# A state-space layer and a linear attention on one core: one ring for states and products, carries by four, steps re-placed, the chunk loop written out

## The chip, the cores and the metric

The kernel runs on one core of one Trainium2 chip. The metric is the device time of one execution in microseconds (us), median of the runs shown. The core has TensorE (PE, with its weight loads as PEld), VectorE (DVE), ScalarE (ACT), GpSimd (POOL) and SyncE (SP), which here only issues DMAs. Each engine works through its own list of instructions in order and waits on semaphores.

## The reference

Input x is 2 images of 512 channels by 4096 tokens, float32. Two layers follow each other, each added to its input:

```
x = x + mamba(group_norm(x))
x = x + linear_attention(group_norm(x))
```

The first layer, per token t, with 1024 inner channels d and 16 states n:

```
xn = layer_norm(x);  xin, z = split(xn @ in_proj.T)
xs = silu(causal_conv4(xin));  dt, B, C = split(xs @ x_proj.T)
delta = softplus(dt @ dt_proj.T + b)
h[d,n] = exp(delta*A[d,n]) * h[d,n] + delta*xs*B[n]
y[d] = sum_n h[d,n]*C[n] + xs*D
out = (y * silu(z)) @ out_proj.T
```

The second layer is a linear attention with 8 heads of 64. The change does not touch it.

## The kernel before

A chunk is 512 tokens; there are 16 (8 for each image). A tile is 128 of the 1024 inner channels, 8 tiles j in a chunk. For each tile there are 16 steps, one for each state n, so a chunk has 128 steps or slots (slot = 16 j + n). In a step VectorE runs one `tensor_tensor_scan` over the 512 tokens (L685): the state is started from a carry, the last state of the chunk before. Every engine has a function that writes out its list for one chunk (`sync_chunk`, `scalar_chunk`, `vector_chunk`, `gpsimd_chunk`, `tensor_chunk`). In one call of it three chunks meet: `scan` is the recurrence of chunk c, `front` the preparation of chunk c+1 (normalization, input projection, convolution, x projection), `project` the out-projection of chunk c-1. The tuples at the top (`NORM`, `MEAN`, `OUT_MM`, `IN_MM`, `Y_COPY` and so on) say by hand in which slot of a chunk, or in which step of a tile, each of these is placed.

What makes up a step n of a tile:

- ScalarE makes the decay exp(delta A) for step n+2 (L475), into SBUF `da` or into a PSUM bank of the ring of three `x_ps`, and every second step scales the last two states into `carry` (L453, L457 for the last pair of the chunk before).
- The inflow delta xs B of nine of the 16 states comes from PE, four 128-wide float32 products with a diagonal of B (L775), two steps ahead, into an `x_ps` bank. Six states have it from VectorE (L670) and one from POOL (L732), written into the state's own place in `hs`, a ring of four.
- POOL multiplies the state by its row of C into `hc`, a second ring of four (L739).
- PE sums the products over n by transposes that add up in the bank `y_ps` (L870), three steps behind (`SUM_LAG`).

Around these, once per tile: ScalarE copies the finished y out of its bank (L581), PE turns it back into an `x_ps` bank (L753), VectorE adds the skip (L642), POOL multiplies by silu(z) (L724). PE makes z with four products (L838), ScalarE its tanh (L585), VectorE the silu (L636). The softplus of the next tile's delta runs on ScalarE (L550 to L569) and POOL (L698 to L707), the turned product du on POOL, PE and ScalarE (L717, L760, L573). Once per chunk: the load of x (L481), group norm and layer norm of the next chunk (L488 to L513, L595 to L611, L784, L791), the input projection and convolution of 8 tiles (L806, L520 to L534, L621, L627), the x projection (L814), the out-projection of 4 channel tiles with 8 products each (L856) and its residual (L652). All float32 products run as two instructions of the same size. SP stores the B and C rows and loads them back, spread over partitions (`b_rows`, `c_rows`) or as diagonals (`b_diag`), when the last tile has used the old ones.

The chunks are ordered by `chunk_loop`: chunks -1, 0, 15 and 16 are written out, 1 to 14 are a loop on every engine:

```
body(engine, 0, True, True, False)
with engine.Fori(1, CHUNKS - 1) as c:
    body(engine, c, True, True, True)
body(engine, CHUNKS - 1, True, False, True)
```

Of the kernel before, what the change touches and what calls it, by code (L numbers as in the profile page):

```python
# [8 lines left out]
ACT = mybir.ActivationFunctionType  # L9
# [14 lines left out]
H_RING, HC_RING, X_RING = 4, 4, 3  # L24
SUM_LAG = 3
# [10 lines left out]
Y_AFTER, DU_AFTER = 5, 11  # L36
# [7 lines left out]
def scans_before(n):  # L44
# [88 lines left out]
def mamba_and_linear_attention(nc, x, ln_w, ln_b, in_proj, conv_w, conv_b, x_proj, dt_proj, dt_b, a_log, d_skip,  # L133
# [10 lines left out]
    with outer:  # L144
# [11 lines left out]
        with layer0:  # L156
# [12 lines left out]
            eps = sb("eps", [P, 1], layer0)  # L169
            keep_now = sb("keep_now", [P, 2], layer0)  # L170
            units = sb("units", [P, 2], layer0)
            one, minus_one = units[:, 0:1], units[:, 1:2]
# [21 lines left out]
            hs = sb("hs", [P, H_RING, T], layer0)  # L194
            hc = sb("hc", [P, HC_RING, T], layer0)
# [9 lines left out]
            squares = (sq[:, :], raw[:, 0:T])  # L205

# [169 lines left out]
            def chunk_loop(body):  # L376

                def on(engine):
                    body(engine, -1, False, True, False)
                    body(engine, 0, True, True, False)  # L380
                    with engine.Fori(1, CHUNKS - 1) as c:
                        body(engine, c, True, True, True)
                    body(engine, CHUNKS - 1, True, False, True)
                    body(engine, CHUNKS, False, False, True)
                return on

            with ExitStack() as main:
# [56 lines left out]
                def scalar_chunk(act, c, scan, front, project):  # L444
                    f = c + 1
                    for j in range(JT):
                        for n in range(STATE):
                            tile, slot = JT * c + j, STATE * j + n
                            step = STEPS * c + slot
                            if scan and n % 2 == 0 and slot > 0:  # L450
                                col = slot - 2
                                act.wait_ge(h_ready, step)
                                act.activation(carry[:, col:col + 2], hs[:, col % H_RING:col % H_RING + 2, T - 1],  # L453
                                               ACT.Copy, scale=keep_now[:, 0:1]).then_inc(carried, 1)
                            if scan and slot == 0 and not (isinstance(c, int) and c == 0):
                                act.wait_ge(h_ready, step)
                                act.activation(carry[:, STEPS - 2:STEPS], hs[:, H_RING - 2:H_RING, T - 1], ACT.Copy,  # L457
                                               scale=keep_now[:, 0:1]).then_inc(carried, 1)
                            if (scan or front) and j == 0 and n == 0:
                                wait(act, carried, STEPS // 2 * c)  # L460
# [17 lines left out]
                            if front and slot == 0:  # L478
                                wait(act, z_mm, JT * c)
                                settle(act, act_fence)  # L480
                                act.dma_start(xn[:, f % 2, :, :], x_v[f // CB, f % CB]).then_inc(x_loaded, 16)  # L481
# [105 lines left out]
                def vector_chunk(dve, c, scan, front, project):  # L587
                    f = c + 1
                    for j in range(JT):
                        for n in range(STATE):  # L590
# [67 lines left out]
                            def pairs_done(back):  # L658
                                return STEPS // 2 * c + (slot + back) // 2 + 1

                            if scan and n + 1 in BY_VECTOR:
# [648 lines left out]
```

## Time and profile before

| | before |
|---|---|
| median of 3 runs | 5244.64 us (5226.87 to 5246.55) |
| profiled execution, its own time | 5233.07 us |
| its span | 5231.1 us |
| mean granted clock of TensorE | 0.965 |
| busy: PE, DVE, ACT, POOL | 87%, 74%, 67%, 72% of the span |

Busy shares are means over everything, the second layer too, in which VectorE and POOL do little. A matmul's end is modelled, so the spacing of the starts says more than the duration. Idle time is put down to the engine that came last, and "issue" is time in which the engine waited for nothing that the profile shows.

### The profile page before, as it was taken

Reading aid. Unit: us, or ns where it says so; the run is one execution under the profiler, and the core shown is the slowest. Engines: PE = TensorE matmul, PEld = TensorE weight load, DVE = VectorE, ACT = ScalarE, POOL = GpSimd, SP = SyncE. Lnnn points to the kernel's source line nnn. Section 1 sums busy time; section 2 is a strip of 40 time slices with the busy share of each in tenths; the row PEclk is TensorE's granted clock in tenths of the full one; section 3 lists DMA queues with packets and bytes.
Section 4 is the critical chain, followed back from the end, with each engine's and each line's share of the span. In section 5 each row is a group of like instructions: output and inputs, shape, how many; then the busy total and the mean of one; then the engine's idle time right before and its main releaser. Section 6 shows DMA issues by size and latency. Waiting matters only on the chain. (4 is left out here: it accounts for less than half of the span.)

```text
span 5231.1 us, 88902 instructions
## 1 busy us (share of the span) xinstructions
PE 4528.0 (87%) x25304; PEld 3301.3 (63%) x25304; DVE 3861.5 (74%) x4157; ACT 3494.4 (67%) x6211; POOL 3782.1 (72%) x3035
## 2 busy tenths in 40 slices
PE   1688989898989898989898989889898998898998
PEld 0366666666666666666666666666666676586786
DVE  4598979888888888888888897979797998212211
ACT  1577777676767777777777776767676776563653
POOL 1388888888787888888878787878787899332322
PEclk9899999999999999999999999999999999999999
DMA  5202020202020202020202011020202020322313
GB/s 210 74 1 82 9 83 9 83 9 83 9 81 11 79 13 79 13 79 13 79 13 68 24 50 40 24 68 4 88 4 88 4 79 9 123 65 97 105 57 113
DMA packets 277100, 290.30 MB, mean 55 GB/s; under 512 B 87376, under 2 KB 166864, under 8 KB 274992
## 3 DMA queue, kind: packets, MB, share of 16 engines
q1 hardware_dynamic: 268080, 266.91, 16.2%
q10 hardware_dynamic: 8448, 16.78, 0.9%
q8 instruction: 235, 3.85, 0.3%
q14 instruction: 337, 2.76, 0.2%
HBM read 246.38 MB, written 37.26 MB: 54 GB/s over the span
## 5 line engine op out<-in xcount | busy, mean ns | idle before, releaser
L739 POOL TENSOR_TENSOR hc<-hs,c_rows 128x512 f32<-128x512 f32 x2048 | 2589.6, 1279 | 707.2 <-DVE hs L685 473.5
L775 PE MATMUL bank<-b_diag,du_t 128*128 128x128 f32 x9216 | 1285.2, 284 | 349.0 <-DVE hs L685 325.1
L685 DVE TENSOR_TENSOR_SCAN hs<-da,carry,bank 128x512 f32<-128x512 f32 x1152 | 1465.7, 1272 | 159.9 <-PE bank L775 85.8
L870 PEld LDWEIGHTS bank<-identity,hc 128*128 128x128 f32 x8192 | 1008.3, 143 | 707.3 <-issue 580.6
L775 PEld LDWEIGHTS bank<-b_diag,du_t 128*128 128x128 f32 x9216 | 1147.7, 196 | 430.5 <-DVE hs L685 391.4
L870 PE MATMUL bank<-identity,hc 128*128 128x128 f32 x8192 | 1232.8, 277 | 50.8 <-ACT sp_l L581 33.9
L685 DVE TENSOR_TENSOR_SCAN hs<-bank,carry,hs 128x512 f32<-128x512 f32 x896 | 1118.7, 1266 | 18.6 <-ACT bank L475 12.2
L475 ACT ACTIVATE da<-delta,neg_a 128x512 f32<-128x512 f32 x1152 | 822.7, 714 | 298.4 <-DVE hs L685 296.9
L475 ACT ACTIVATE bank<-delta,neg_a 128x512 f32<-128x512 f32 x896 | 612.2, 683 | 207.1 <-DVE hs L685 205.1
L670 DVE TENSOR_TENSOR hs<-bank,b_rows 128x512 f32<-128x512 f32 x768 | 520.4, 678 | 119.7 <-ACT carry L453 93.6
L856 PE MATMUL bank<-xs,w_out 128*128 (+1 forms) x1024 | 539.0, 631 | 67.7 <-issue 65.4
L1041 POOL TENSOR_TENSOR xg_low<-xg,xg_high 128x512 fp32r<-128x512 f32 x192 | 248.4, 1294 | 481.3 <-ACT xg_high L1065 473.7
L453 ACT ACTIVATE carry<-hs,keep_now 128x2 f32<-128x2 f32 x1008 | 294.1, 292 | 419.2 <-DVE hs L685 418.1
L806 PE MATMUL bank<-xn,w_in 128*128 (+1 forms) x1024 | 524.3, 598 | 23.6 <-DVE xs L627 12.4
L838 PE MATMUL bank<-xn,w_in 128*128 (+1 forms) x1024 | 529.3, 599 | 0.0
L856 PEld LDWEIGHTS bank<-xs,w_out 128*128 128x128 f32 x1024 | 191.4, 204 | 229.1 <-issue 223.7
L621 DVE SCALAR_TENSOR_TENSOR bank<-raw,w_conv,bank 128x512 f32<-128x512 f32 x384 | 288.5, 751 | 54.4 <-ACT bank L526 45.3
L698 POOL TENSOR_TENSOR sp_w<-sp_w,sp_e 128x512 f32<-128x512 f32 x128 | 163.3, 1275 | 170.3 <-ACT sp_w L565 168.9
L838 PEld LDWEIGHTS bank<-xn,w_in 128*128 128x128 f32 x1024 | 177.4, 193 | 126.1 <-issue 126.1
L1065 ACT ACTIVATE xg<-xl,gn_bias,gn_scale 128x512 f32<-128x512 f32 x192 | 155.0, 807 | 143.5 <-DMA xl<-x 131.8
L1154 DVE COPY ek_t<-l_bank 128x512 f32<-128x512 f32 x64 | 44.3, 692 | 219.1 <-PE l_bank L1229 219.1
L642 DVE SCALAR_TENSOR_TENSOR xs<-xs,skip,bank 128x512 f32 (+1 forms) x128 | 94.6, 739 | 133.8 <-PE bank L753 133.7
(159 smaller groups left out, 5909.9 us busy)
## 6 DMA issues: line engine op xcount, KB each, us to landing
c_rows<-b_and_c_rows SPq DMA_DIRECT2D x256, 256.0 KB, 7.3
xl<-x SPq DMA_DIRECT2D x48, 1024.0 KB, 5.5
b_diag<-b_diagonals SPq DMA_DIRECT2D x144, 256.0 KB, 7.2
b_rows<-b_and_c_rows SPq DMA_DIRECT2D x112, 256.0 KB, 7.1
c_rows<-in_x SPq DMA_DIRECT2D x8, 2048.0 KB, 8.4
xn<-in_x ACTq DMA_DIRECT2D x16, 1024.0 KB, 9.1
xres<-in_x SPq DMA_DIRECT2D x64, 256.0 KB, 3.2
x<-xres SPq DMA_DIRECT2D x64, 256.0 KB, 2.1
```

What stands on the lines that cost most here:

```text
L453: act.activation(carry[:, col:col + 2], hs[:, col % H_RING:col % H_RING + 2, T - 1], ACT.Copy, scale=keep_now[:, 0:1]).then_inc(carried, 1)
L475: act.activation(da[:, nn % X_RING, :] if nn in BY_TENSOR else x_ps[ring_bank(nn)][:, :], delta[:, jn % 2, :], ACT.Exp, scale=neg_a[:, jn, ...
L621: dve.scalar_tensor_tensor(in_ps[t][:, :], raw[:, TAPS - 1 - s:TAPS - 1 - s + T], w, in_ps[t][:, :], ALU.mult, ALU.add).then_inc(conv_step, 1)
L670: dve.tensor_tensor(hs[:, nn % H_RING, :], du_ps[:, :], b_rows[:, v, :], ALU.mult).then_inc(dbu_ready, 1)
L685: dve.tensor_tensor_scan(hs[:, n % H_RING, :], decay, inflow, carry[:, STATE * j + n:STATE * j + n + 1], ALU.mult, ALU.add).then_inc(h_rea ...
L739: pool.tensor_tensor(hc[:, n % HC_RING, :], hs[:, n % H_RING, :], c_rows[:, n, :], ALU.mult).then_inc(hc_ready, 1)
L775: mm = pe.matmul(x_ps[ring_bank(nn)][:, q * P:(q + 1) * P], du_t[:, jn % 2, q * P:(q + 1) * P], b_diag[:, w, q, :], start=True, stop=True)
L806: mm = pe.matmul(in_ps[t][:, :], w_in[:, ct, t * P:(t + 1) * P], xn[:, f % 2, ct, :], start=ct == 0, stop=ct == CT - 1)
L838: mm = pe.matmul(pb[:, :], w_in[:, ct, lo:lo + P], xn[:, c % 2, ct, :], start=ct == 0, stop=ct == CT - 1)
L856: mm = pe.matmul(pout[:, :], w_out[:, k, ct * P:(ct + 1) * P], xs[:, o % 2, k, :], start=k == 0, stop=k == JT - 1)
L870: mm = pe.matmul(y_ps[:, q * P:(q + 1) * P], hc[:, ns % HC_RING, q * P:(q + 1) * P], identity[:, :], start=ns == 0 and q == 0, stop=ns == ...
L1041: pool.tensor_tensor(xg_parts[1][:, u, ct, :], xg[:, ct % 2, :], xg_parts[0][:, u, ct, :], ALU.subtract).then_inc(lowered, 1)
```

## The change

- One ring `hs` of eight places of 513 columns holds states and products. The state lies in columns 1 to 512; POOL writes the product with C over it, in columns 0 to 511. The last state stays readable in column 512 for the carry. `hc` goes. VectorE and POOL now wait, before they write a state or an inflow, for the sum (`n_summed`) of the state eight steps before, where they waited for its product; POOL waits for nothing but the state before it writes a product.
- Carries are copied by four, every fourth step, in place of by two.
- The sums stand four steps behind, those of n = 0 and 1 together in step 5. The copy of y, the turn back, the skip and the gate move from steps 3, 4, 6, 9 to 4, 7, 9, 10; the tanh and silu of z from 11, 12 to 12, 14; the softplus one step later.
- The load of x moves to slot 122 of the chunk before; the normalization to slots 0 to 3, and what follows it some slots earlier.
- Seven of the eight products of the first channel tile of the out-projection move into slots 112 to 124 of the chunk itself.
- The loop over chunks 1 to 14 is written out; each wait then names a constant.
- `eps` becomes a third column of `units`.

```diff
-H_RING, HC_RING, X_RING = 4, 4, 3
-SUM_LAG = 3
+H_RING, X_RING, CARRIES = 8, 3, 4
-Y_AFTER, DU_AFTER = 5, 11
+Y_AFTER, DU_AFTER = 8, 11
-NORM, MEAN, CENTER = (3, 4, 6, 7), (6, 8, 11, 12), 15
-SQUARE, VARIANCE = (17, 20), (18, 19, 21, 22)
-RSTD, NEWTON, SCALE, AFFINE = 24, 26, 27, 28
-OUT_MM = ((0, 0, 1, 3, 5, 6, 9, 10), (13, 16, 16, 18, 19, 21, 23, 24), (28, 29, 29, 32, 32, 35, 35, 38),
-          (42, 44, 45, 48, 48, 51, 51, 54))
-OUT_ADD = (12, 27, 41, 57)
-IN_MM = ((39, 41, 42, 44), (53, 54, 55, 57), (59, 60, 61, 62), (65, 66, 67, 68), (70, 71, 73, 74), (76, 77, 78, 80),
-         (82, 83, 84, 86), (88, 89, 90, 92))
+X_LOAD = STEPS - 6
+NORM, MEAN, CENTER = (0, 1, 2, 3), (3, 4, 5, 6), 8
+SQUARE, VARIANCE = (9, 11), (11, 12, 13, 15)
+RSTD, NEWTON, SCALE, AFFINE = 17, 19, 20, 21
+OUT_FIRST = (112, 112, 115, 115, 118, 121, 124)
+OUT_MM = ((None,) * 7 + (13,), (16, 16, 18, 19, 19, 21, 22, 24), (27, 28, 31, 31, 32, 34, 35, 37),
+          (41, 42, 44, 45, 47, 48, 50, 51))
+OUT_ADD = (15, 26, 39, 53)
+IN_MM = ((35, 38, 38, 39), (48, 50, 51, 51), (54, 55, 57, 58), (60, 61, 63, 64), (66, 67, 69, 70), (73, 74, 76, 77),
+         (80, 80, 83, 83), (86, 87, 89, 90))
-X_MM, DBL, DT_SPLIT = (94, 95, 96, 96, 97, 98, 99, 100), 102, 104
-DT_MM, SP_ABS, SP_EXP, SP_ROUND, SP_LN, SP_REST, SP_SUM, SP_DELTA = 14, 0, 0, 2, 4, 3, 5, 6
+X_MM, DBL, DT_SPLIT = (93, 93, 95, 96, 96, 98, 99, 100), 102, 104
+DT_MM, SP_ABS, SP_EXP, SP_ROUND, SP_LN, SP_REST, SP_SUM, SP_DELTA = 15, 1, 1, 3, 5, 4, 6, 7
-Z_MM, Z_TANH, Z_SILU = (2, 3, 6, 9), 11, 12
-Y_COPY, Y_BACK, Y_SKIP, Y_GATE = 3, Y_AFTER - 1, Y_AFTER + 1, 9
+Z_MM, Z_TANH, Z_SILU = (2, 3, 6, 9), 12, 14
+Y_COPY, Y_BACK, Y_SKIP, Y_GATE = 4, Y_AFTER - 1, Y_AFTER + 1, 10
+SUMS = {4 + max(ns, 1): (ns,) if ns > 1 else (0, 1) for ns in range(STATE)}
...
-            hs = sb("hs", [P, H_RING, T], layer0)
-            hc = sb("hc", [P, HC_RING, T], layer0)
+            hs = sb("hs", [P, H_RING, T + 1], layer0)
+            def state(n):
+                return hs[:, n % H_RING, 1:]
+            def weighted(n):
+                return hs[:, n % H_RING, 0:T]
...
-                    with engine.Fori(1, CHUNKS - 1) as c:
+                    for c in range(1, CHUNKS - 1):
                         body(engine, c, True, True, True)
...
-                            if scan and n % 2 == 0 and slot > 0:
-                                col = slot - 2
+                            if scan and n % CARRIES == 0 and step > 0:
+                                col = (slot - CARRIES) % STEPS
                                 act.wait_ge(h_ready, step)
-                                act.activation(carry[:, col:col + 2], hs[:, col % H_RING:col % H_RING + 2, T - 1],
-                                               ACT.Copy, scale=keep_now[:, 0:1]).then_inc(carried, 1)
...
+                                act.activation(carry[:, col:col + CARRIES],
+                                               hs[:, col % H_RING:col % H_RING + CARRIES, T], ACT.Copy,
                                                scale=keep_now[:, 0:1]).then_inc(carried, 1)
...
-                            if front and slot == 0:
-                                wait(act, z_mm, JT * c)
+                            g = f if c < 0 and slot == 0 else f + 1
+                            if g < CHUNKS and (c < 0 and slot == 0 or slot == X_LOAD):
+                                wait(act, z_mm, JT * (g - 1))
...
-                                wait(dve, hc_ready, step + 2 - H_RING)
-                                wait(dve, carried, pairs_done(1 - H_RING))
-                                dve.tensor_tensor(hs[:, nn % H_RING, :], du_ps[:, :], b_rows[:, v, :],
+                                wait(dve, n_summed, step + 2 - H_RING)
+                                wait(dve, carried, carries_done(1 - H_RING))
+                                dve.tensor_tensor(state(nn), du_ps[:, :], b_rows[:, v, :],
...
-                                    wait(dve, hc_ready, step + 1 - H_RING)
-                                    wait(dve, carried, pairs_done(-H_RING))
+                                    wait(dve, n_summed, step + 1 - H_RING)
+                                    wait(dve, carried, carries_done(-H_RING))
...
-                                wait(pool, n_summed, step + 1 - HC_RING)
-                                pool.tensor_tensor(hc[:, n % HC_RING, :], hs[:, n % H_RING, :], c_rows[:, n, :],
+                                pool.tensor_tensor(weighted(n), state(n), c_rows[:, n, :],
...
+                            for k in range(JT - 1) if scan else ():
+                                if slot != OUT_FIRST[k]:
+                                    continue
...
+                                pe.wait_ge(gated, JT * c + k + 1)
+                                pe.matmul(pout[:, :], w_out[:, k, 0:P], xs[:, c % 2, k, :], start=k == 0, stop=False)
...
-                            js, ns = (j, n - SUM_LAG) if n >= SUM_LAG else (j - 1, n - SUM_LAG + STATE)
-                            if scan if js >= 0 else project:
+                            for ns in (*SUMS.get(n, ()), *SUMS.get(n + STATE, ())):
+                                js = j if n > ns else j - 1
```

## Rows read from the trace of the kernel before

**Rows 1.** The page's first line.

```profile
span 5231.1 us, 88902 instructions
```

**Rows 2.** Source lines L462 (first chunks) and L457 (later starts): first, last start.

```profile
L462 ACT ACTIVATE keep_now<-keep x2: 188/196/204, 88.2 to 189.5; 128x2 f32<-128x2 f32 x2
...
L457 ACT ACTIVATE carry<-hs,keep_now x15: 296/297/298, 457.1 to 4217.6; 128x2 f32<-128x2 f32 x15
```

**Rows 3.** Stretches by chunk: length, busy PE PEld DVE ACT POOL, clock, DMA, GB/s.

```profile
457.30:3955.80 3498.50, 3112.26 (x18006) 2240.98 (x18006) 2977.05 (x3109) 2504.19 (x4512) 2851.24 (x2289) 0.97 0.15 45
...
3955.80:4217.90 262.10, 238.24 (x1384) 171.45 (x1383) 227.98 (x239) 192.66 (x347) 218.11 (x176) 0.97 0.12 38
...
4217.90:4440.00 222.10, 198.03 (x1297) 152.22 (x1296) 197.59 (x201) 156.15 (x278) 214.79 (x174) 1.00 0.08 25
```

**Rows 4.** Who waited for whom, VectorE, whole run: total us, times, longest us.

```profile
DVE xs L642 <- PE bank L753: 133.7, 77, 5.7
DVE zs L636 <- ACT zs L585: 133.5, 97, 2.3
DVE hs L670 <- ACT carry L453: 93.6, 91, 2.3
DVE hs L685 <- PE bank L775: 85.8, 84, 29.2
DVE hs L685 <- issue: 64.7, 19, 5.3
```

**Rows 5.** Who waited for whom, POOL and PE, whole run.

```profile
POOL hc L739 <- PE bank L870: 216.0, 220, 4.8
...
PE bank L870 <- ACT sp_l L581: 33.9, 30, 4.1
```

**Rows 6.** Timeline of VectorE at a chunk boundary: start, duration, idle before.

```profile
993.63 1.28 DVE L685 TENSOR_TENSOR_SCAN hs<-da,carry,bank 128x512 f32<-128x512 f32 x1 [4.90 <-issue]
```

**Rows 7.** Stretches after that boundary, columns as in rows 3.

```profile
995.00:1000.00 5.00, 4.81 (x9) 2.59 (x10) 3.89 (x4) 3.39 (x8) 2.60 (x3) 0.50 1.03 351
1002.00:1040.00 38.00, 34.40 (x193) 23.75 (x193) 29.73 (x30) 25.40 (x46) 29.71 (x25) 1.00 0.05 19
```

**Rows 8.** Waits of VectorE in chunk 15 alone.

```profile
DVE hs L685 <- issue: 0.4, 1, 0.4
```

**Rows 9.** Groups of instructions by line, whole run: busy us, mean ns | idle before.

```profile
L739 POOL TENSOR_TENSOR hc<-hs,c_rows 128x512 f32<-128x512 f32 x2048 | 2589.6, 1279 | 707.2 <-DVE hs L685 473.5 <-PE bank L870 216.0 <-issue 11.0
...
L453 ACT ACTIVATE carry<-hs,keep_now 128x2 f32<-128x2 f32 x1008 | 294.1, 292 | 419.2 <-DVE hs L685 418.1
...
L724 POOL TENSOR_TENSOR xs<-xs,zs 128x512 f32 (+1 forms) x128 | 163.9, 1281 | 3.0 <-DVE xs L642 3.0
...
L826 PE MATMUL bank<-dt_rows,w_dt 96*128 96x512 f32 x128 | 78.3, 612 | 2.0 <-DVE dt_rows L632 2.0
```

**Rows 10.** Two source lines of VectorE: duration ns, min/median/max.

```profile
L621 DVE SCALAR_TENSOR_TENSOR bank<-raw,w_conv,bank x384: 728/756/757, 126.7 to 4162.2; 128x512 f32<-128x512 f32 x192
...
L642 DVE SCALAR_TENSOR_TENSOR xs<-xs,skip,bank x128: 720/746/749, 247.0 to 4438.1; 128x512 f32 x112, 128x512 f32<-128x512 f32 x16
```

**Rows 11.** Timelines of POOL and PE: start, duration, count merged.

```profile
983.73 3.74 POOL L739 TENSOR_TENSOR hc<-hs,c_rows 128x512 f32<-128x512 f32 x3
...
1000.92 0.60 PE L870 MATMUL bank<-identity,hc 128*128 128x128 f32 x4
1001.36 1.06 PE L775 MATMUL bank<-b_diag,du_t 128*128 128x128 f32 x8
1002.25 1.02 PE L838 MATMUL bank<-xn,w_in 128*128 x2
1003.12 0.60 PE L870 MATMUL bank<-identity,hc 128*128 128x128 f32 x4
```

**Rows 12.** The load of x: issues and landing from the page; ScalarE's wait.

```profile
xn<-in_x ACTq DMA_DIRECT2D x16, 1024.0 KB, 9.1
...
ACT xn L488 <- DMA xn<-in_x: 44.5, 14, 5.7
```

More of the change, by code:

```diff
@@ L168, in mamba_and_linear_attention @@
             channel_mean = sb("channel_mean", [P, P], layer0)
[L169 removed]
             keep_now = sb("keep_now", [P, 2], layer0)
[L171 to L172 removed]
+            units = sb("units", [P, 3], layer0)
+            one, minus_one, eps = units[:, 0:1], units[:, 1:2], units[:, 2:3]
             keep = sb("keep", [P, CHUNKS + 2], layer0)
@@ L449, in scalar_chunk @@
                             step = STEPS * c + slot
-                            if scan and n % 2 == 0 and slot > 0:
-                                col = slot - 2
+                            if scan and n % CARRIES == 0 and step > 0:
+                                col = (slot - CARRIES) % STEPS
                                 act.wait_ge(h_ready, step)
-                                act.activation(carry[:, col:col + 2], hs[:, col % H_RING:col % H_RING + 2, T - 1],
-                                               ACT.Copy, scale=keep_now[:, 0:1]).then_inc(carried, 1)
-                            if scan and slot == 0 and not (isinstance(c, int) and c == 0):
-                                act.wait_ge(h_ready, step)
-                                act.activation(carry[:, STEPS - 2:STEPS], hs[:, H_RING - 2:H_RING, T - 1], ACT.Copy,
+                                act.activation(carry[:, col:col + CARRIES],
+                                               hs[:, col % H_RING:col % H_RING + CARRIES, T], ACT.Copy,
                                                scale=keep_now[:, 0:1]).then_inc(carried, 1)
                             if (scan or front) and j == 0 and n == 0:
-                                wait(act, carried, STEPS // 2 * c)
+                                wait(act, carried, STEPS // CARRIES * c)
                                 wait(act, halo_saved, JT * f)
@@ L656, in vector_chunk, with carries_done @@
                                              xres[:, ct % 2, :]).then_inc(x2_stat, 1)
-                            def pairs_done(back):
-                                return STEPS // 2 * c + (slot + back) // 2 + 1
+                            def carries_done(back):
+                                return STEPS // CARRIES * c + (slot + back) // CARRIES + 1
                             if scan and n + 1 in BY_VECTOR:
@@ L729, in gpsimd_chunk @@
                                     pool.wait_ge(b_loaded[ROWS.index(nn)], 16 * (c + 1))
-                                wait(pool, hc_ready, step + 3 - H_RING)
-                                wait(pool, carried, STEPS // 2 * c + (slot + 2 - H_RING) // 2 + 1)
-                                pool.tensor_tensor(hs[:, nn % H_RING, :], du[:, :], b_rows[:, ROWS.index(nn), :],
+                                wait(pool, n_summed, step + 3 - H_RING)
+                                wait(pool, carried, STEPS // CARRIES * c + (slot + 2 - H_RING) // CARRIES + 1)
+                                pool.tensor_tensor(state(nn), du[:, :], b_rows[:, ROWS.index(nn), :],
                                                    ALU.mult).then_inc(pool_dbu, 1)
@@ L850, in tensor_chunk @@
                                         pe.wait_ge(x2_ready, CT * o + ct)
-                                    if k == 0 and ct == 0:
-                                        if scan:
-                                            pe.wait_ge(dt_split, c + 1)
-                                        else:
-                                            pe.wait_ge(x2_ready, CT * o)
                                     mm = pe.matmul(pout[:, :], w_out[:, k, ct * P:(ct + 1) * P], xs[:, o % 2, k, :],
@@ L869, in tensor_chunk @@
                                 for q in range(BLOCKS):
-                                    mm = pe.matmul(y_ps[:, q * P:(q + 1) * P],
-                                                   hc[:, ns % HC_RING, q * P:(q + 1) * P], identity[:, :],
-                                                   start=ns == 0 and q == 0, stop=ns == STATE - 1,
+                                    mm = pe.matmul(y_ps[:, q * P:(q + 1) * P], weighted(ns)[:, q * P:(q + 1) * P],
+                                                   identity[:, :], start=ns == 0 and q == 0, stop=ns == STATE - 1,
                                                    is_transpose=True, skip_group_check=True)
```

17 lines of the change are left out of this document (11 added, 6 removed).

## The prediction

> **What bounds the kernel now.** I read the page first for the span, then the stretches by chunk, then who waits for whom, then three short timelines. The profiled execution took 5233.07 us; its span is 5231.1 us [rows 1]. The sum below is made against this execution; the median of the runs shown, 5244.64 us, lies 12 us above it.
>
> Chunk 0 starts at 189.5 us and the last of the 15 later starts is at 4217.6 us [rows 2]; chunk 15 is over by 4440, and nothing that the change touches comes much later. So some 4250 us of the span are 16 chunks of 8 tiles of 16 steps. The 13 chunks from 457.3 to 3955.8 us take 269.1 us each; divided by 13, VectorE is busy 229.0 us in one, PE 239.4, POOL 219.3 and ScalarE 192.6 [rows 3]. No engine alone is the bound: three lie within 10% of each other and at least 30 us a chunk go to waits. The reader should see that the shares don't name a bound here; the waits must.
>
> VectorE's scans are the chain that everything else follows. Over the run it waits 133.7 us for the y that PE turns back (L753), 133.5 us for the tanh of z (L585), 93.6 us for carries, 85.8 us for PE's inflow (L775), and 64.7 us for "issue" [rows 4]. POOL waits 216.0 us for PE's sums, which free its four product buffers, and PE 33.9 us for the copy of y [rows 5].
>
> **The loop.** At a boundary, VectorE's first scan of the new iteration comes at 993.63 us after 4.90 us of "issue" [rows 6]; no data that it needs is late. This is the back edge. The other engines stand too, and from 995 to 1000 us PE's granted clock is 0.50, the lower level of 1.2 GHz; from 1002 to 1040 us, with PE at work, it is 1.00 [rows 7]. The price is had without a model: the last loop iteration has no back edge behind it and takes 262.1 us [rows 3], 7.0 us under the mean of the 13 that have one. Unrolled, 13 x 7.0 = 91 us go. What straight-line code pays is seen where the code already stands outside the loop: in all of chunk 15, VectorE's "issue" is 0.4 us [rows 8].
>
> The Trainium skill, page Runtime: NRT & Kernel Launch, section Instruction fetch mechanics, says that a taken branch to a target outside the fetched window stalls until that code is read, while straight-line code is streamed ahead. The trace agrees: 4.90 us at the back edge against 0.4 us in all of chunk 15. By that rule alone only the stall is saved, 13 x 4.9 = 64 us, and the sum would be 27 us smaller; I keep the measured 7.0 us.
>
> **The y chain.** Now the 16th sum of a tile is PE's at step 2 of the next, its copy ScalarE's at step 3, PE's first sum of the new tile also at step 3, the turn back at step 4, the skip VectorE's at step 6. Each has a step or less for what another engine must finish. After: last sum at 3, copy at 4, no sum in step 4, two sums in step 5, turn at 7, skip at 9. VectorE's 133.7 us and PE's 33.9 us [rows 4, 5] lose their reason. The tanh of z and its use get two steps between them in place of one: the 133.5 us come in 97 waits of 1.4 us [rows 4], less than a step of 2.1 us (269.1 / 128).
>
> **Carries.** A carry costs 292 ns for two numbers a partition [rows 9]. One of four lies between that and twice as much; I take 0.3, as two more numbers are nothing beside 512. 511 in place of 1023 then save 150 us of ScalarE, which is no bound and gains nothing by it. What counts is VectorE's wait: with a ring of four, the inflow written at step s needs a pair that ScalarE may copy only at step s-1; with eight, a group of four copied at s-3 or before. The 93.6 us [rows 4] go unless ScalarE is three steps late.
>
> **The ring of eight, products in place.** The products are written one column to the left over their own state. POOL no longer waits for PE's sums before it writes a product, 216.0 us [rows 5], and PE has four steps before it needs one. VectorE takes over the wait for buffers, but for sums of step s-7, which PE orders at s-3; queued behind it are the inflow or scan of that step and all later ones, and POOL, ScalarE and PE wait for those. PE can't be three steps late, since VectorE would stand for its inflow first: priced at nothing. The odd start costs VectorE nothing as a reader: L621 reads at offsets 0, 1 and 2 in 728 to 757 ns, the same form without offset, L642, takes 720 to 749 [rows 10]. POOL and PE have no such row. Nearest is POOL's exact in-place product L724, 1281 ns against 1279 for L739 [rows 9]; I take zero, and as the upper end a second pass, 1279 ns more for each of 2048.
>
> **The re-placed steps.** By the spacing of starts at full clock, a sum costs PE 0.44 us, an inflow of eight matmuls 0.89, a 512-wide product 0.87 [rows 11]. A bare tile is 9 x 0.89 + 18 x 0.44 (sums and turns) + 4 x 0.87 (z) + 0.6 (dt, L826 [rows 9]) = 20.0 us. The 80 further products of a chunk (means, variances, in, x and out projections) fall on the eight tiles as 13, 14, 12, 13, 11, 11, 6, 0 before and 9, 12, 13, 14, 9, 11, 5, 7 after, since seven of the first out-projection go into the last tile. POOL has 22 instructions a tile at 1.247 us (three in 3.74 [rows 11]): 27.4. VectorE, with 1.2 us a scan and 0.62 an inflow, chosen so that a chunk comes to its 229 us, has 27.9, 30.8, 25.6, 30.5, 32.4, 30.3, 27.0, 24.2 before, and 27.9, 30.8, 28.4, 30.5, 30.3, 31.8, 24.9, 24.2 after. The largest of the three, tile by tile, is 31.3 + 32.2 + 30.5 + 31.3 + 32.4 + 30.3 + 27.4 + 27.4 = 242.8 us before and 27.9 + 30.8 + 31.3 + 32.2 + 30.3 + 31.8 + 27.4 + 27.4 = 239.1 after. The chunk without back edge, 262.1, stands 19.3 us above its 242.8. Of VectorE's waits, y, z and carries are (133.7 + 133.5 + 93.6) / 16 = 22.6 us in the mean chunk, PE's inflow 5.4, and what then remains of 269.1 - 229.0 without the 4.9 of the loop is 7.2. After, I put these 7.2 and a third of the 5.4, since the full tiles of PE are in the bound already, on top of 239.1: 248 us.
>
> The x load moves from step 0 to step 122 of the chunk before, on ScalarE's queue, into the time when rows and diagonals fill the DMA engines (busy share 1.03 at 995 us [rows 7]). It lands 9.1 us after its issue, and ScalarE waited 44.5 us for it in all [rows 12], 2.8 a chunk; six steps of 1.9 us are 11.4, so this wait nearly goes. But the normalizations now share steps 0 to 3 with the softplus: decays of that tile, and PE's first z product behind the ReLU, are late next. I set one against the other, with 2.8 us a chunk, 45 in all, as bound on either side.
>
> **Sum.** 13 x (269.1 - 248) = 274; the last loop iteration 262.1 - 248 = 14; chunk 0, with less of PE's work, 12; chunk 15, where POOL is busy 214.8 of 222.1 us [rows 3], 1. Together 301: 5233 - 301 = 4932, and with a part of the 12 us to the median **4940 us**.
>
> **Rivals.** (a) The removed waits come back: the three x banks stay, PE is never more than two steps ahead, and in the tiles of 31 and 32 us VectorE waits for L775 where it waited for y. For it: PE is busy 239 of 269 us. At 257 us a chunk, 13 x 12 + 5 + 6 = 167: 5070; with the loop alone 5140. (b) All fits, to 240 us a chunk: 13 x 29 + 22 + 18 + 2 = 419: 4815. Against it: two engines near their limit must meet at every step. (c) Slower: POOL takes longer for a product written one column from where it is read. A chunk is then 48 x 1.247 + 128 p; it reaches today's mean of 4250 / 16 = 266 us at p = 1.61 us, 29% more. With the second pass, p = 2.53, it is 383 us and the kernel 5233 + 16 x 117 = 7100. No row speaks for it, the in-place L724 against. (d) Straight-line code stalls at DMA-filled boundaries as the back edge did, and the other waits return: no change, 5220 to 5250.
>
> **How the numbers follow.** Forecast, 4840 to 5010: 0.65. Rival (a), 5010 to 5140: 0.20. (b): 0.06. (d): 0.04. (c): 0.05. The range 4840 to 5110 leaves out (b), (c), (d) and the upper end of (a), about 0.2; the 45 us of the x load lie within it. Within 0.5% is what a measurement of this kernel can't tell from no change. Faster 0.91, same 0.04, slower 0.05.
>
> **What would show it.** Chunk starts 248 us apart; no "issue" near 5 us, and clock 1.00 over the boundaries; VectorE's waits for L753, L585 and carries near zero, that for L775 no larger than now; POOL's product at 1279 ns (above 1.6 us the ring is what went wrong); ScalarE's wait for x gone. If starts lie 257 us apart or more, what VectorE waits for in the first six tiles names the step that failed.

## The result, and the profile after

The changed kernel takes 5153.15 us (5151.01 to 5154.95), the kernel before 5240.93 in the runs that stand for this comparison: a ratio of 0.9841, 95% interval 0.9823 to 0.9859. It is faster, by 88 us and not by 300, and lies 43 us above the upper end of the range. The sum gave 248 us a chunk; it is (3877.7 - 464.4) / 13 = 262.6, almost the 262.1 that chunk 14 took before without a back edge behind it [rows 3], and chunk 14 itself stays where it was. The first line of the page, then stretches by chunk (columns as in [rows 3]) and a boundary:

```profile
span 5149.3 us, 73875 instructions
```

```profile
464.40:3877.70 3413.30, 3084.74 (x17994) 2234.47 (x17993) 2966.08 (x3108) 2430.46 (x4095) 2687.36 (x2289) 0.98 0.15 45
3877.70:4139.10 261.40, 234.95 (x1386) 170.57 (x1385) 228.03 (x240) 186.91 (x315) 206.62 (x177) 0.99 0.15 45
...
4139.10:4355.00 215.90, 192.83 (x1286) 150.96 (x1284) 196.97 (x200) 149.75 (x244) 201.63 (x173) 1.00 0.08 27
...
984.00:996.00 12.00, 9.42 (x65) 7.45 (x64) 12.00 (x14) 9.44 (x17) 11.99 (x12) 1.00 1.08 359
```

The last stretch holds the start of chunk 3. The back edge of [rows 6, 7] is gone: VectorE is busy all 12 us and the clock is 1.00, though the DMA engines are as full as before. Of the 82 us between the two spans, the 13 chunks give 85.2 and chunk 15 6.2; chunk 0 takes some 4 more.

So nearly all that the rest of the change was to bring must have been given back. VectorE's waits (total us, times, longest), then ScalarE's, POOL's and PE's:

```profile
DVE hs L690 <- issue: 130.4, 120, 2.3
DVE hs L690 <- PE bank L779: 106.3, 96, 28.8
DVE xres L657 <- PE bank L864: 100.3, 49, 8.7
...
DVE hs L675 <- PE bank L879: 53.3, 57, 1.8
DVE zs L641 <- ACT zs L590: 44.6, 15, 3.3
...
DVE xs L647 <- PE bank L757: 3.7, 1, 3.7
...
ACT sp_l L586 <- PE bank L879: 307.9, 113, 6.7
...
POOL delta L707 <- ACT sp_e L574: 248.7, 122, 5.0
...
PE bank L779 <- DVE hs L690: 352.4, 331, 2.8
```

Two lines of the kernel before stand beside these:

```profile
DVE xres L652 <- PE bank L856: 33.6, 18, 6.5
...
ACT sp_l L581 <- PE bank L870: 60.8, 58, 4.8
```

Against [rows 4, 5], the waits for y (133.7 to 3.7) and carries (93.6 to nothing) went, that for z fell from 133.5 to 44.6, and POOL's product no longer waits for PE. In their place VectorE waits 237 us for PE's inflow: L779 by name, and "issue", which is PE's list too where a timeline below looks into it. ScalarE, which waited 60.8 us for the last sum of a tile, waits 307.9. And VectorE's wait for the last product of an out-projection, before it adds the residual (L657), grew from 33.6 to 100.3.

### The profile page after: what moved, and what is told of

Its sections match the earlier page's. It is cut to its first block and busy times, and to the rows that moved or that the text cites. A ratio compares the mean times of both kernels' runs of the same rounds, so it can differ in the third digit from the quotient of the medians.

```text
span 5149.3 us, 73875 instructions
## 1 busy us (share of the span) xinstructions
PE 4506.6 (88%) x25304; PEld 3299.9 (64%) x25304; DVE 3851.6 (75%) x4157; ACT 3403.2 (66%) x5699; POOL 3582.7 (70%) x3035
## 5 line engine op out<-in xcount | busy, mean ns | idle before, releaser
L743 POOL TENSOR_TENSOR hs<-hs,c_rows 128x512 f32<-128x512 f32 x2048 | 2386.6, 1184 | 577.2 <-DVE hs L690 563.6
L779 PE MATMUL bank<-b_diag,du_t 128*128 128x128 f32 x9216 | 1260.6, 282 | 373.4 <-DVE hs L690 352.4
L779 PEld LDWEIGHTS bank<-b_diag,du_t 128*128 128x128 f32 x9216 | 1129.4, 194 | 474.7 <-DVE hs L690 348.8
L879 PEld LDWEIGHTS bank<-identity,hs 128*128 128x128 f32 x8192 | 1000.7, 143 | 587.2 <-issue 521.6
L879 PE MATMUL bank<-identity,hs 128*128 128x128 f32 x8192 | 1184.8, 275 | 2.2 <-POOL hs L743 2.2
L842 PE MATMUL bank<-xn,w_in 128*128 128x512 f32 x1024 | 558.3, 628 | 51.3 <-ACT delta L559 51.3
L675 DVE TENSOR_TENSOR hs<-bank,b_rows 128x512 f32<-128x512 f32 x768 | 521.3, 679 | 55.2 <-PE bank L879 53.3
L810 PE MATMUL bank<-xn,w_in 128*128 128x512 f32 x1024 | 527.5, 611 | 23.1 <-DVE xs L632 12.1
L864 PE MATMUL bank<-xs,w_out 128*128 128x512 f32 x800 | 411.6, 610 | 4.7 <-DVE xres L657 2.3
L707 POOL TENSOR_TENSOR delta<-delta,sp_e 128x512 f32<-128x512 f32 x128 | 162.3, 1268 | 248.8 <-ACT sp_e L574 248.7
L842 PEld LDWEIGHTS bank<-xn,w_in 128*128 128x128 f32 x1024 | 182.6, 200 | 180.7 <-issue 123.9
L703 POOL TENSOR_TENSOR sp_w<-sp_w,sp_e 128x512 f32<-128x512 f32 x128 | 162.7, 1271 | 191.9 <-ACT sp_w L570 191.9
L586 ACT ACTIVATE sp_l<-bank 128x512 f32<-128x512 f32 x128 | 76.3, 596 | 308.0 <-PE bank L879 307.9
L864 PEld LDWEIGHTS bank<-xs,w_out 128*128 128x128 f32 x800 | 144.9, 197 | 121.5 <-issue 112.0
L810 PEld LDWEIGHTS bank<-xn,w_in 128*128 128x128 f32 x1024 | 167.5, 198 | 73.4 <-issue 44.2
```

The source lines that it names most:

```text
L675: dve.tensor_tensor(state(nn), du_ps[:, :], b_rows[:, v, :], ALU.mult).then_inc(dbu_ready, 1)
L743: pool.tensor_tensor(weighted(n), state(n), c_rows[:, n, :], ALU.mult).then_inc(hc_ready, 1)
L779: mm = pe.matmul(x_ps[ring_bank(nn)][:, q * P:(q + 1) * P], du_t[:, jn % 2, q * P:(q + 1) * P], b_diag[:, w, q, :], start=True, stop=True)
L810: mm = pe.matmul(in_ps[t][:, :], w_in[:, ct, t * P:(t + 1) * P], xn[:, f % 2, ct, :], start=ct == 0, stop=ct == CT - 1)
L842: mm = pe.matmul(pb[:, :], w_in[:, ct, lo:lo + P], xn[:, c % 2, ct, :], start=ct == 0, stop=ct == CT - 1)
L864: mm = pe.matmul(pout[:, :], w_out[:, k, ct * P:(ct + 1) * P], xs[:, o % 2, k, :], start=k == 0, stop=k == JT - 1)
```

## The experiments

A ratio is to the kernel before on the same chip, with its 95% interval. Edits are against the changed kernel unless another is named. The order is that of the argument.

**The loop alone**, in the kernel before, and **the change with its loop kept**:

```diff
-                    with engine.Fori(1, CHUNKS - 1) as c:
+                    for c in range(1, CHUNKS - 1):
```

> The kernel before, with nothing changed but the chunk loop, which is written out. Theory A (the whole gain of 1.6% is the loop; all else trades waits for waits on PE's inflow): 13 x 7.0 us = 91 us less than before, ratio 0.980 to 0.985, 5135 to 5165 us. Theory B (the ring, the carries and the re-placed steps bring part of it, and written-out code pays something of its own): 20 to 60 us less than before, ratio above 0.988.

> The changed kernel with the chunk loop put back for chunks 1 to 13 (chunk 14 written out, 12 back edges). Theory A: the back edges cost their 7.0 us again, 12 x 7 = 84 us, so about the time of before, ratio 0.997 to 1.003. Theory B: clearly faster than before, ratio under 0.993.

The loop alone: 5159.59 us, 0.9854 [0.9823, 0.9884], all that the whole change gives. The change with a loop of 13 iterations: 5233.0, 0.999 [0.9978, 1.0003]. Twelve back edges cost 80 us, 6.7 each, and everything else together comes to nothing within the intervals. Is it nothing part by part, or do gains and losses cancel?

**The ring and the carries**, added to the loop-only kernel, with sums three behind and all placements as before:

```diff
-H_RING, HC_RING, X_RING = 4, 4, 3
+H_RING, X_RING, CARRIES = 8, 3, 4
...
+SUMS = {ns + 3: (ns,) for ns in range(STATE)}
```

> The kernel before with the loop written out, the ring of eight with products in place and carries by four; sums three behind and every placement as before. VectorE's waits for carries, 6 to 7 us a chunk, must go. If they are real cost, 90 to 110 us less than with the loop alone: 5050 to 5070 us, ratio about 0.967. If they come back as waits for y and PE, 5110 to 5160 us, ratio 0.976 to 0.986.

5111.28, 0.9768 [0.9738, 0.9799]: a gain of 48 us over the loop alone. In the loop-only kernel VectorE waited 89.1 us for carries; that is gone, and for PE's inflow, "issue" with it, it waits 107 in place of 81. First the loop-only kernel, then this one:

```profile
DVE hs L670 <- ACT carry L453: 89.1, 88, 2.4
DVE hs L685 <- PE bank L775: 42.7, 48, 27.7
...
DVE hs L685 <- issue: 38.2, 53, 2.4
```

```profile
DVE hs L687 <- issue: 53.7, 53, 2.3
DVE hs L687 <- PE bank L776: 53.6, 78, 29.2
```

**Only y, z and softplus moved**, added to that, with sums three behind; **sums three behind** in the changed kernel, which differs from it by the front, the load of x and the out-projection. The line of the second is:

```diff
-SUMS = {4 + max(ns, 1): (ns,) if ns > 1 else (0, 1) for ns in range(STATE)}
+SUMS = {3 + max(ns, 2): (ns,) if ns > 2 else (0, 1, 2) for ns in range(STATE)}
```

> The kernel with ring and carries (loop written out) plus the y, z and softplus steps as changed and sums three behind; front, x load and out-projection as before. It differs from the changed kernel with sums three behind (5057 us) in the front and the out-projection alone. If these bring nothing, as waits there trade against each other, 5040 to 5075 us; if spreading PE's work over the chunk boundary brings what the tile maxima say, 3.7 us a chunk, 5100 us or more.

> The changed kernel with the sums three steps behind, those of n = 0, 1, 2 together in step 5, so that the last sum stands at step 2 and its copy two steps later, at step 4. Theory C (ScalarE's wait for that sum is the new limit): ScalarE's 307.9 us fall under 100, and the time by 50 us or more, ratio to before under 0.975. Theory A: ScalarE's wait falls, the time stays within 0.5% of the changed kernel's 5153 us, ratio 0.979 to 0.989.

The first: 5127.9, 0.9789 [0.9763, 0.9814]; the moves that were to free 267 us of waits for y and z bring nothing beside the kernel of 5111. The waits did fall, y from 138.7 to 47.1 us and z from 152.2 to nothing, but one for ScalarE's decays came in their place:

```profile
DVE hs L687 <- ACT da L477: 109.6, 31, 5.7
```

All but 1 us of it stands in slots 6 and 22, beside the old steps of the normalization and its squares, for which ScalarE first waits 81.2 us for x. So the moves were tried beside a front that took their gain away, and what a part is worth depends on the order in which the parts are added.

The second: 5056.62, 0.9651 [0.9624, 0.9678]. Added last, the front, the load of x and the out-projection in their new places are thus worth 71 us, and the sums in theirs cost 97. Of the kernels here that leave no work out, none is faster. ScalarE's wait for the last sum fell from 307.9 to 40.3 us; VectorE's for the residual stays:

```profile
DVE hs L690 <- issue: 160.2, 192, 2.5
DVE xres L657 <- PE bank L864: 108.1, 49, 8.9
...
DVE hs L690 <- PE bank L779: 39.8, 37, 28.3
DVE hs L675 <- PE bank L879: 37.4, 46, 1.8
...
ACT sp_l L586 <- PE bank L879: 40.3, 61, 7.1
...
POOL delta L707 <- ACT sp_e L574: 74.2, 62, 2.6
```

A tile of the changed kernel shows what ScalarE stood for. Timeline of PE, ScalarE and VectorE: start, duration, count merged, idle before:

```profile
1427.06 1.92 PE L779 MATMUL bank<-b_diag,du_t 128*128 128x128 f32 x8 [2.02 <-DVE hs L690]
1428.77 1.91 PE L842 MATMUL bank<-xn,w_in 128*128 128x512 f32 x2
1430.48 0.70 PE L879 MATMUL bank<-identity,hs 128*128 128x128 f32 x4
1431.02 1.88 PE L810 MATMUL bank<-xn,w_in 128*128 128x512 f32 x4
1432.74 1.02 PE L842 MATMUL bank<-xn,w_in 128*128 128x512 f32 x2
1433.59 0.60 PE L879 MATMUL bank<-identity,hs 128*128 128x128 f32 x4
1434.03 1.95 PE L779 MATMUL bank<-b_diag,du_t 128*128 128x128 f32 x16
...
1434.23 0.60 ACT L586 ACTIVATE sp_l<-bank 128x512 f32<-128x512 f32 x1 [3.35 <-PE bank L879]
...
1435.18 1.28 DVE L690 TENSOR_TENSOR_SCAN hs<-da,carry,bank 128x512 f32<-128x512 f32 x1 [2.28 <-issue]
```

Step 2 of the tile ends with the sum at 1430.48. Step 3 has two products of the input projection and one of z ahead of the last sum, so that one comes 3.1 us later, at 1433.59, and ScalarE stands 3.35 us for it with its decays and the softplus of the next tile behind the copy. Over the run this wait is not spread evenly: it is 76 us in the list of tile 3, whose step 3 has three products besides that of z, and 7 in that of tile 4, which has one. The 2.28 us of "issue" on VectorE end when the first of the two inflows from 1434.03 is done: PE, with nothing late but its own list.

**Is it the lag of four, or a gap of one step?** In the changed kernel one step lies between the last sum (3) and its copy (4). A kernel with **four behind and the copy later** gives it two:

```diff
-Y_COPY, Y_BACK, Y_SKIP, Y_GATE = 4, Y_AFTER - 1, Y_AFTER + 1, 10
-SUMS = {4 + max(ns, 1): (ns,) if ns > 1 else (0, 1) for ns in range(STATE)}
+Y_COPY, Y_BACK, Y_SKIP, Y_GATE = 5, Y_AFTER - 1, Y_AFTER + 1, 10
+SUMS = {4 + max(ns, 2): (ns,) if ns > 2 else (0, 1, 2) for ns in range(STATE)}
```

> The changed kernel with the sums still four steps behind, but those of n = 0, 1, 2 together in step 6 and the copy of y at step 5, two steps after the last sum in place of one. If the cost of the changed kernel is ScalarE standing for the last sum (theory C), this brings what three behind brought: 5040 to 5080 us. If the cost is the lag of four itself (VectorE standing for sums that free its places), 5140 to 5160 us.

5162.04, 0.986 [0.9838, 0.9882]: no gain, although ScalarE's wait fell to 13.1 us. VectorE's wait for sums grew to 199.6 us:

```profile
DVE hs L675 <- PE bank L879: 199.6, 106, 3.5
...
ACT sp_l L586 <- PE bank L879: 13.1, 16, 6.7
```

That looked like the lag itself. But of the six inflows that VectorE writes in a tile, all of this wait stands before the third, n = 8 (by the order of the 768 in the timeline). It takes the place of n = 0, and the edit had moved that sum to step 6, one step before the inflow of step 7: another gap of one step. Three more runs, all against sums three behind, take lag and gap apart:

```diff
 # three behind, copy in the next step
-Y_COPY, Y_BACK, Y_SKIP, Y_GATE = 4, Y_AFTER - 1, Y_AFTER + 1, 10
+Y_COPY, Y_BACK, Y_SKIP, Y_GATE = 3, Y_AFTER - 1, Y_AFTER + 1, 10
 # three behind, first sums late
+SUMS = {3 + max(ns, 3): (ns,) if ns > 3 else (0, 1, 2, 3) for ns in range(STATE)}
 # four behind, caught up
+SUMS = {5: (0, 1, 2), **{ns + 4: (ns,) for ns in range(3, 13)}, 17: (13, 14), 18: (15,)}
```

> Sums three behind, as in the 5057 us kernel, but the copy of y in step 3, one step after the last sum, as in the changed kernel. Theory G (what costs is a gap of a single step between a sum and the engine that waits for it): about 5150 us, and ScalarE waits about 300 us for the last sum. Theory L (what costs is that the sums run four behind, whatever the gaps): 5050 to 5070 us.

> Sums three behind, the copy two steps after the last sum, but the first four sums of a tile together in step 6, one step before VectorE's inflow takes the place of the first state. Theory G: 5120 to 5170 us, and VectorE waits 150 to 200 us for that sum, as where the first three of sums four behind stood in step 6 (199.6 us, 5162 us). Theory L: 5050 to 5070 us, with that wait near the 37 us of the 5057 us kernel, or a longer wait that costs nothing.

> The first three sums in step 5, those of n = 3 to 13 four or more steps behind, the last two caught up so that the last is done at step 2 and the copy stays two steps after it; no consumer has a gap of less than two steps. Theory G: 5050 to 5075 us, like sums three behind. Theory L: 5120 to 5160 us.

Copy in the next step: 5078.99, 0.9686 [0.9659, 0.9713], between the two theories, with a wait of ScalarE of 98.8 us and not 300. First sums late: 5133.97, 0.9792 [0.9762, 0.9823], as theory G said, with VectorE's wait for sums at 177.3 us, again all before the third inflow. Four behind, caught up: 5061.07, 0.9654 [0.9625, 0.9684], the same as three behind. The lines are of the first two:

```profile
ACT sp_l L586 <- PE bank L879: 98.8, 72, 7.1
```

```profile
DVE hs L675 <- PE bank L879: 177.3, 95, 3.5
```

So the lag of four is free, and the changed kernel pays for the place of few sums: with those of 14, 15 and 2 one step earlier it is 92 us faster. A gap of one step can cost, but it has no price of its own: 77 us at the first sum, 22 at the copy with the sum in step 2 and the copy in 3 (the intervals touch), some 90 with the sum in step 3 and the copy in 4. Theory G had 90 for both of the last two, and the kernel before had the gap of the first of them with a wait of 60.8 us. Why step 3 is so much dearer than step 2 was not tested; the products ahead of the sum there are a part of it, by the tiles above. The granted clock doesn't order these kernels: its mean is 0.969 in the changed one, 0.970 with the copy in the next step, 74 us faster, and 0.980 with four behind and the copy later, the slowest.

**What limits now: less work on one engine.** One z product of four is left (three quarters of z are left out), in the changed kernel and in the loop-only kernel; then the taps s = 2 and 3 of the convolution are cut to 8 of 512 columns (most of their sums are left out):

```diff
+                                if ct < CT - 1:
+                                    continue
...
```

```diff
+                                        m = T if s == 1 else 8
...
```

> The changed kernel with one of the four z products of a tile (the other three are left out), 24 x 0.87 = 20.9 us of PE less in a chunk; nothing else differs. If PE, in order and two steps ahead, is what holds VectorE (theory A), at least half comes off, 10 us a chunk, so 5000 us or less, and VectorE's waits for the inflow with issue fall from 237 us to under 120. If ScalarE's wait for the last sum (307.9 us) makes decays late and that holds VectorE (theory C), under 3 us a chunk, so above 5100 us.

> The kernel before with the loop written out and one of the four z products of a tile (three left out), the same 20.9 us of PE less in a chunk that took 12.4 us a chunk off the changed kernel. If the kernel before is held by its chains (y, tanh of z, carries) and not by PE, clearly less comes off: under 6 us a chunk, above 5070 us. If PE held it as it holds the changed one, 12 us a chunk, under 4970 us.

> The changed kernel with two of the three convolution taps of VectorE cut to 8 columns (most of their sums left out): 16 instructions of about 0.67 us less for VectorE in a chunk, 10.7 us. If PE and ScalarE alone hold the chunk, under 3 us of that come off, above 5105 us. If VectorE's own work still counts in full, 10 us a chunk, 5000 us; halves of both, 5050 us.

Without 24 products, 24 x 0.87 = 20.9 us of PE a chunk [rows 11], the changed kernel falls to 4955.54, 0.9459 [0.9425, 0.9493], by 12.3 us a chunk (198 / 16), the loop-only kernel to 5123.14, 0.9785 [0.975, 0.982], by 2.3. VectorE's two waits for the inflow fall from 237 to 117:

```profile
DVE hs L690 <- issue: 74.9, 99, 1.5
...
DVE hs L690 <- PE bank L779: 42.0, 42, 28.8
...
ACT sp_l L586 <- PE bank L879: 113.6, 58, 6.7
```

The kernel before was held by its chains more than by PE, the changed one is held by PE. Two things blur the comparison. The pages' busy times, of the changed kernel and without z, then of the loop-only kernel and without z, show that PE's fell by 321 us in the one and by 238 in the other:

```profile
PE 4506.6 (88%) x25304; PEld 3299.9 (64%) x25304; DVE 3851.6 (75%) x4157; ACT 3403.2 (66%) x5699; POOL 3582.7 (70%) x3035
PE 4186.0 (84%) x24536; PEld 3157.1 (64%) x24536; DVE 3838.9 (77%) x4157; ACT 3398.6 (69%) x5699; POOL 3581.1 (72%) x3035
PE 4503.7 (88%) x25304; PEld 3298.0 (64%) x25304; DVE 3848.9 (75%) x4157; ACT 3489.9 (68%) x6211; POOL 3779.1 (73%) x3035
PE 4265.4 (83%) x24536; PEld 3219.5 (63%) x24536; DVE 3839.0 (75%) x4157; ACT 3496.5 (68%) x6211; POOL 3776.4 (74%) x3035
```

In the loop-only kernel the mean granted clock fell with the z products, from 0.969 to 0.950, so PE gave part of its relief back; in the changed kernel it is 0.969 and 0.971. And a z product stands ahead of the last sum in step 3, so ScalarE's wait for that sum fell too, from 307.9 to 113.6 us. Of the 198 us only the 101 by which 4956 lies under three behind (5057) are beyond what the place of the sums is worth.

The changed kernel is held by VectorE as well: with two taps cut, 5008.33, 0.9566 [0.9531, 0.96], 145 us less, about all that its busy time falls by (3851.6 to 3722.3 us, 129):

```profile
PE 4473.6 (89%) x25304; PEld 3279.1 (65%) x25304; DVE 3722.3 (74%) x4157; ACT 3404.4 (68%) x5699; POOL 3583.6 (72%) x3035
```

**The head of the chunk**: normalization back to its steps of before, in sums three behind:

```diff
-NORM, MEAN, CENTER = (0, 1, 2, 3), (3, 4, 5, 6), 8
+NORM, MEAN, CENTER = (3, 4, 6, 7), (6, 8, 11, 12), 15
...
```

> The changed kernel with sums three behind and the normalization back in its old slots (3, 4, 6, 7 and on), with x loaded early as changed. If the crowding of ScalarE in steps 0 to 3 costs (VectorE's 44.6 us for the tanh of z, PE's 48.2 us behind the ReLU), 30 us or more under 5057 us. If that is hidden, within 0.5% of 5057 us.

5067.53, 0.9678 [0.9657, 0.9699] against 5056.62: the crowded head costs nothing. VectorE's wait for decays, 109.6 us where y and z were moved beside the old front, is 0.2 here with the old normalization and the early load of x, which points to that load or to the out-projection; no run has the one without the other.

**Freer banks**, in sums three behind: all decays in SBUF, so that the three x banks hold inflows and turns alone, given out in PE's order:

```diff
...
+                                    decay, inflow = da[:, step % X_RING, :], state(n)
...
```

> The changed kernel with sums three behind and all decays in SBUF, so that the three x banks serve PE's inflows and the two turns alone, each wait being for the use three before; PE may then run further ahead of the scans in most steps. If PE's short lead is what makes VectorE wait for inflows (issue and L779, 200 us there, theory A), these waits halve and the time is 60 us or more under 5057 us. If a scan with both inputs in SBUF is slower than 1.27 us, or the lead isn't it, 5050 us or above.

5275.64, 1.0073 [1.0049, 1.0097], 219 us above three behind. VectorE's waits for the inflow are nearly gone as wanted (31.4 and 15.4), but the scans that read both inputs from SBUF took longer:

```profile
L706 DVE TENSOR_TENSOR_SCAN hs<-da,carry,hs 128x512 f32<-128x512 f32 x896 | 1507.2, 1696 | 127.7 <-POOL hs L753 88.8 <-ACT da L495 38.4
L706 DVE TENSOR_TENSOR_SCAN hs<-da,carry,bank 128x512 f32<-128x512 f32 x1152 | 1455.4, 1263 | 73.0 <-PE bank L801 31.4 <-ACT da L495 25.9 <-issue 15.4
...
L706 DVE TENSOR_TENSOR_SCAN hs<-da,carry,hs x896: 1248/1570/2381, 211.3 to 4475.7; 128x512 f32<-128x512 f32 x180
```

The last line has their minimum, median and maximum: the shortest take no longer than those with one input in PSUM. The time goes where they meet POOL. The 51 beside which POOL ran nothing took 1273 to 1277 ns. Of POOL's products, those that met no such scan took 1091 or 1273 ns in the mean, by step as in the last section, and those that lay beside one for 1 us or more 1927 or 2132.

896 x (1.696 - 1.263) = 388 us more of VectorE. Without them it would be some 4890 us, an estimate that counts them in full; no run here shows that kernel.

**Padding**, in sums three behind: two columns more in front of a state and between states, for POOL's product (see the last section):

```diff
-            hs = sb("hs", [P, H_RING, T + 1], layer0)
+            hs = sb("hs", [P, H_RING, T + 4], layer0)
...
-                return hs[:, n % H_RING, 1:]
+                return hs[:, n % H_RING, 2:T + 2]
...
```

> The changed kernel with sums three behind, and places of 516 columns with the state from column 2 and the product from column 1, so that state, product and row of C start at three different positions modulo four in every place; the small tiles of the first group norm move into the tile of z to make room. If POOL's product depends on these positions, all 2048 take 1.09 us, where half took 1.27. If it depends on the place in the ring, half stay at 1.27. The time stays within 0.5% of the 5057 us without it, if POOL is no bound; 30 us or more below if it is.

5059.8, 0.966 [0.9633, 0.9687]: the same time, with every product faster. POOL isn't the bound.

## Why the prediction was right, and where it failed

**The loop: right.** 91 us were forecast, 77 measured alone (5237 against 5160) and 80 the other way round. VectorE stood 4.0 to 5.3 us before its first scan behind each of the 13 back edges, 61 in all, where the prediction took 4.9 for each. The Trainium skill, page Runtime: NRT & Kernel Launch, section Instruction fetch mechanics, says that a taken branch to a target outside the fetched window stalls. By that stall alone the prediction had 64 us; the interval of the loop alone, 61 to 93 us, reaches this and the forecast.

**The waits for y, z, carries and x: right as waits, wrong as time.** All fell as said. A carry of four takes 293 ns, one of two 292. ScalarE's wait for x is 9.2 us (44.5 before [rows 12]). As time, added in this order, they are worth 48 us with ring and carries (of a wait of 89), nothing for y and z, 71 for the front, x and out-projection together; of this the slots of the normalization are at most a little (5068 against 5057 us), and the rest was not separated.

**The step that failed: "VectorE's 133.7 us and PE's 33.9 us lose their reason", and with it the sum that takes the 22.6 us a chunk of waits for y, z and carries off and puts nothing in their place.** I gave the copy and everything after it more room, and did not look at what now stands before the copy: the last sum moved to step 3, behind that step's products on PE, and its copy to the step after it. The wait went from VectorE to ScalarE (60.8 to 307.9 us), and behind ScalarE to the softplus (POOL waits 248.7 us for it, 74.2 with sums three behind). It cost 92 to 97 us, 6 a chunk, of the 213 between 4940 and 5153. That the places of states come free in time, "priced at nothing", holds in the main (53.3 us of waits, of which 37.4 stay in the faster kernel), but with the first sums a step later it fails, by 77 us.

**The second term, the other 117 us: 9 us above the largest engine of each tile.** With the sums in place a chunk takes 256.5 us ((3789.3 - 455.4) / 13, from the first scans of chunks 1 and 14), 17.3 above the 239.1 and not 9. By the first scans of each tile, chunks 2 to 12, the eight tiles take 33.4, 34.5, 32.1, 37.2, 31.1, 33.9, 27.5 and 26.6 us; the sum had 27.9, 30.8, 31.3, 32.2, 30.3, 31.8, 27.4 and 27.4. The last two meet it, in part by luck: their 27.4 was POOL's, whose products take 1186 ns in the mean here and not the 1279 that I kept. Tiles 0, 1 and 3 miss it by 4 to 6. In tile 3 the wait for the residual stands, which no term had: of the 108.1 us, 70.6 are for the fourth channel tile, 4.4 a chunk. Its last product and its residual had moved from slots 54 and 57 to 51 and 53, two steps apart in place of three; no run tests what that costs. I had kept a third of the wait for PE's inflow, since PE's full tiles were in the bound already. It grew instead: with "issue", from 5.1 us a chunk in the loop-only kernel ((42.7 + 38.2) / 16) to 12.5 ((160.2 + 39.8) / 16). By the kernel's order, with three x banks, PE makes an inflow only two steps ahead, itself waits for the scan that frees the bank (292 us), and then has up to three products of 0.87 us in its list before the next. Rival (a) said this, "the removed waits come back", with 5140 where they come back whole, and 5153 lies just above; I gave it 0.20. That PE's lead is what is short, and not its sum of work, is not shown: leaving out z takes from both, and where the banks were freer VectorE itself was slower, which gave PE time. That more banks bring time was not shown either, since that kernel paid elsewhere.

**Right at nothing:** the crowded head (+11 us with the old one, within the intervals) and straight-line code at the boundary (rival (d)). The odd start of the state, priced at zero with a longer product as the risk (rival (c)), made POOL's product shorter, 1184 ns in the mean, which brought no time.

## What to carry to other kernels

When several engines stand near their limit, a wait that disappears from one engine's list is worth what the next chain behind it leaves, here between nothing and half of it; test each move on the chip before adding their waits up, and know that its worth depends on which others are in place. When a step is moved, follow both of its ends: what stands ahead of it in its own engine's list in the new slot, and how many steps remain to each consumer, as a few sums one step too late cost up to 97 us where a longer lag for all the others cost nothing. A change that nets to zero can hide a good one: one line of placement separates 5153 from 5057 us.

## What the runs showed of the hardware that I had not expected

The time of POOL's product of two float32 operands depends on where its operands start. In the changed kernel it has two levels, 1091 to 1095 ns in steps with n mod 4 = 1 or 2 and 1271 to 1280 in the others (means of each step over 128 tiles), where before all took 1275 to 1282. With 513 columns a place, state, product and C row start at three different places modulo four numbers just in the fast steps; in the others, and in the kernel before, two or all of them agree (by the kernels' indices). With 516 columns a place they differ in every step, and all are fast (1093 to 1099), so it isn't the place in the ring. Minimum, median and maximum of the changed and the padded kernel:

```profile
L743 POOL TENSOR_TENSOR hs<-hs,c_rows x2048: 1077/1199/1331, 207.6 to 4353.0; 128x512 f32<-128x512 f32 x187
```

```profile
L742 POOL TENSOR_TENSOR hs<-hs,c_rows x2048: 1081/1095/1129, 205.5 to 4262.1; 128x512 f32<-128x512 f32 x187
```

A scan with decay and inflow both in SBUF takes 1696 ns in the mean, 1263 with one in PSUM, and POOL's products in the same kernel 1423 where they took 1186; where the two don't meet, neither is longer (1273 to 1277, and 1091 or 1273). The Trainium skill, page GPSIMD Engine Reference, section 1. Specifications, says that GpSimd's way to SBUF is shared with VectorE and contended by its instructions with two SBUF inputs; the trace agrees, and shows that either side can pay.

In the tile shown above, the inflow at 1427.06 took 1.92 us, and with sums three behind the same one, at 1402.88, took 1.16. That is the clock: the granted clock is 0.57 there, mostly the lower level, and 1.00 in the other kernel (columns as in [rows 3]; first the changed kernel):

```profile
1427.00:1431.00 4.00, 3.94 (x14) 2.80 (x15) 4.00 (x6) 3.84 (x7) 3.75 (x4) 0.57 0.00 0
```

```profile
1402.80:1406.80 4.00, 3.92 (x18) 2.53 (x19) 4.00 (x6) 3.94 (x8) 3.73 (x4) 1.00 0.00 0
```

PE had stood 2.02 us before either; why the clock fell in the one alone, no run tells.
